# Order of the first layer norm's statistics and of the graph convolution's evacuations in a four-stage graph network kernel

## What is computed

```
L0  h = x @ fc^T + b;  8 Euler steps  h += dt*(alph*0.5*(adj@h - h) + h@w_eff - h + x)
L1  h = relu(adj @ (x @ Wg0 + bg0)); h = relu(adj @ (h @ Wg1 + bg1))
    for p in 1..4: an LSTM over windows of p nodes overwrites every p-th node of h
L2  A_hat = normalised adj; batchnorm(relu(batchnorm((A_hat @ x) @ W1^T + b1)) @ W2^T + b2)
L3  edge attention with 4 heads over 256 edges (segment softmax), then @ W_out^T
```

## Time and profile before

| what | value |
|---|---|
| median of 3 runs | 1010.1 us (1010.0 to 1010.34) |
| profiled execution, its own time | 1015.05 us |
| its span, first to last instruction | 1013.0 us |
| mean granted clock of TensorE | 0.969 |
| HBM traffic | 22.83 MB read, 7.87 MB written |

### The profile page before, as it was taken

One profiled execution on the slowest core, in us unless ns is written; L12 is line 12 of the kernel. 1 busy time (PEld: TensorE's weight loads), 2 busy tenths in 40 slices (PEclk: granted clock), 3 DMA queues, 4 the chain that ended last, 5 costly groups with the idle time before them and its releaser, 6 DMA issues. The chain is left out here.

```text
span 1013.0 us, 14415 instructions
## 1 busy us (share of the span) xinstructions
PE 926.2 (91%) x5120; PEld 795.4 (79%) x5120; DVE 671.9 (66%) x1662; ACT 538.4 (53%) x1112; POOL 309.3 (31%) x284
## 2 busy tenths in 40 slices
PE   6999997999998999998999999899999978588984
PEld 4689986899997898997889899787788853365763
DVE  6665435445546657655755675697887876779887
ACT  2043324664645565554565564557567548366644
POOL 3011222332323233232323333314333220155742
PEclk9989999999999999999999999999979998799987
DMA  8030011001010100101010001201100000000014
GB/s 223 1 81 17 7 63 63 1 22 42 1 42 2 42 22 1 42 2 42 1 42 21 29 15 35 89 1 63 42 1 22 2 0 1 0 1 1 0 44 123
DMA packets 33995, 31.62 MB, mean 31 GB/s; under 512 B 8451, under 2 KB 28035, under 8 KB 33925
## 3 DMA queue, kind: packets, MB, share of 16 engines
q1 hardware_dynamic: 32900, 30.64, 9.9%
q10 hardware_dynamic: 960, 0.07, 0.1%
q0 software_dynamic: 64, 0.00, 0.0%
HBM read 22.83 MB, written 7.87 MB: 30 GB/s over the span
## 5 line engine op out<-in xcount | busy, mean ns | idle before, releaser
L1322 ACT ACTIVATE gates<-psum,gbias 128x256 f32<-128x256 f32 (+2 forms) x312 | 158.9, 566 | 68.5 <-PE psum L67 64.5
L65 PE MATMUL psum<-LS,WI 128*128 128x256 f32 (+2 forms) x312 | 105.0, 337 | 8.9 <-ACT gates L1322 5.3
L67 PE MATMUL psum<-LS,WI 128*128 128x256 f32 (+2 forms) x312 | 103.6, 332 | 0.0
L66 PE MATMUL psum<-LS,WI 128*128 128x256 f32 (+2 forms) x312 | 103.6, 332 | 0.0
L72 POOL TENSOR_TENSOR LS<-A,LS 128x512 fp32r<-128x512 f32 (+2 forms) x44 | 49.0, 1114 | 170.7 <-ACT LS L1307 170.6
L72 POOL TENSOR_TENSOR LS<-Hodd,LS 128x512 fp32r<-128x512 f32 (+2 forms) x44 | 48.6, 1103 | 150.4 <-ACT LS L1307 150.4
L72 DVE TENSOR_TENSOR yl<-psum,yh 128x512 fp32r<-128x512 f32 x58 | 39.6, 688 | 65.1 <-ACT yh L1264 44.0
L72 POOL TENSOR_TENSOR XSl<-X,XSh 128x512 fp32r<-128x512 f32 x32 | 42.6, 1334 | 115.9 <-ACT XSh L1259 115.9
L65 PEld LDWEIGHTS psum<-LS,WI 128*128 128x128 f32 x312 | 59.8, 192 | 18.2 <-POOL LS L72 9.9
L1329 ACT ACTIVATE tc<-cell 128x512 f32<-128x512 f32 (+2 forms) x88 | 45.3, 514 | 53.5 <-DVE cell L1617 29.4
L65 PE MATMUL psum<-B2h,LT2h 128*128 128x256 f32 x256 | 72.7, 284 | 1.0 <-DVE X L1435 1.0
(11 more groups left out here) (372 smaller groups left out, 2680.8 us busy)
## 6 DMA issues: line engine op xcount, KB each, us to landing
WI<-lstm_weights SPq DMA_DIRECT2D x14, 512.0 KB, 3.6
WH<-lstm_weights SPq DMA_DIRECT2D x11, 512.0 KB, 4.6
X<-in_x SPq DMA_DIRECT2D x16, 256.0 KB
out<-X SPq DMA_DIRECT2D x16, 256.0 KB, 2.3
lstm_weights<-WI SPq DMA_DIRECT2D x4, 512.0 KB, 2.6
lstm_weights<-WH SPq DMA_DIRECT2D x3, 512.0 KB, 2.7
A<-in_adj SPq DMA_DIRECT2D x4, 256.0 KB, 4.4
z_A<-in_adj SPq DMA_DIRECT2D x1, 1024.0 KB, 5.3
```

Of the source, the lines that this page charges most:

```text
L65: pe.matmul(out, lhs[0], rhs[0], start=start, stop=False)
L66: pe.matmul(out, lhs[0], rhs[1], start=False, stop=False)
L67: return pe.matmul(out, lhs[1], rhs[0], start=False, stop=stop)
L1322: act.activation(gates[:, gate, 0:n], sh.psum[:, gate, 0:n], ACT.Tanh if gate == G else ACT.Sigmoid, bias=gbias[:, p_ - 1, gate:gate + 1]) ...
```

## The change

The statistics of a pair of batches are taken in halves by node chunks: `("st1", q, a, 0)` now covers chunks 0 and 1 of both batches and stands right behind half 0 of "s"; `("st1", q, a, 1)` covers chunks 2 and 3. In each quarter the second half stands between the layer 0 "v" of batch 0 and its relu. "sh1", the apply of batch 2 and its split move ahead of the first layer 1 product; the apply of batch 3 moves behind the second. In quarter 0 the sets 8 and 9 stand behind both layer 0 "v", set 10 behind both layer 1 "v", set 11 behind the layer 0 "v" of batch 3 and set 12 between the layer 1 "v" of batches 2 and 3. At the end of the order, the statistics of batch 3 and "ln2" of quarter 3's second norm move behind L2's product of batch 11.

```diff
         def giant(kind, q, a):
-            return [(kind, q, a, j) for j in (0, 1)] + ([("th", q, a)] if kind == "t" else [])
+            if kind == "t":
+                return [("t", q, a, 0), ("t", q, a, 1), ("th", q, a)]
+            return [("s", q, a, 0), ("st1", q, a, 0), ("s", q, a, 1)]
...
         def first_norm(q, a):
-            return [("st1", q, a, 0), ("st1", q, a, 1), ("ln1", q, a)]
+            return [("st1", q, a, 1), ("ln1", q, a)]
...
-                    applied(q, 1), split(q, 4), back(q, 3), split(q, 5), giant("t", q, 1), mix(q, 0, 0), mix(q, 1, 0),
-                    giant("s", q, 1), weigh(q, 0, 0), first_norm(q, 1), weigh(q, 1, 0), mix(q, 0, 1), applied(q, 2),
-                    applied(q, 3), split(q, 6), mix(q, 1, 1), split(q, 7), weigh(q, 0, 1), weigh(q, 1, 1), mix(q, 2, 0),
-                    split(q + 1, 0) if q < NQ - 1 else [], mix(q, 3, 0), split(q + 1, 1) if q < NQ - 1 else [],
-                    weigh(q, 2, 0), weigh(q, 3, 0), mix(q, 2, 1), mix(q, 3, 1), weigh(q, 2, 1), weigh(q, 3, 1)]
+                     applied(q, 1), split(q, 4), back(q, 3), split(q, 5), giant("t", q, 1), mix(q, 0, 0), mix(q, 1, 0),
+                     giant("s", q, 1), [("v", q, 0, 0), ("st1", q, 1, 1), ("relu", q, 0), ("ln1", q, 1), ("v", q, 1, 0),
+                                        ("relu", q, 1)]]
+            second = [*applied(q, 2), *split(q, 6)]
+            if q == 0:
+                sets = [[("set", n)] for n in range(NSET - SETS_LATE, NSET)]
+                return parts + [sets[0], sets[1], second, mix(q, 0, 1), mix(q, 1, 1), applied(q, 3), split(q, 7),
+                                weigh(q, 0, 1), weigh(q, 1, 1), sets[2], mix(q, 2, 0),
+                                ahead[0], mix(q, 3, 0), ahead[1], weigh(q, 2, 0), weigh(q, 3, 0), sets[3], mix(q, 2, 1),
+                                mix(q, 3, 1), weigh(q, 2, 1), sets[4], weigh(q, 3, 1)]
+            return parts + [second, mix(q, 0, 1), mix(q, 1, 1), applied(q, 3), split(q, 7), weigh(q, 0, 1), weigh(q, 1, 1), mix(q, 2, 0), ahead[0], mix(q, 3, 0), ahead[1],
+                            weigh(q, 2, 0), weigh(q, 3, 0), mix(q, 2, 1), mix(q, 3, 1), weigh(q, 2, 1), weigh(q, 3, 1)]
...
-            for part in rest:
-                parts.append(part)
-                if part and part[0][0] in ("v", "s"):
-                    parts.append([next(late, None)])
-            parts.append(list(late))
+            parts += rest
...
-        order += applied2(q_, 0, 2) + [("xz", z_)] + widened(z_ - 3) + norm2(q_, 2, 4) + aggregated(z_ - 1)
+        order += applied2(q_, 0, 2) + [("xz", z_)] + widened(z_ - 3) + [("st2", q_, 2)] + aggregated(z_ - 1) + [("st2", q_, 3), ("ln2", q_, 2, 4)]
...
-            def first_stats(q, a, b):
-                if b == 0:
-                    dve.wait_ge(S["ring_free"], ring["s", q, a, 1] + 1)
-                ins = norm.take_stats(dve, QB * q + 2 * a + b)
-                if b == 1:
+            def first_stats(q, a, j):
+                dve.wait_ge(S["ring_free"], ring["s", q, a, j] + 1)
+                for b in (0, 1):
+                    for c in range(2 * j, 2 * j + 2):
+                        ins = norm.row_stats(dve, QB * q + 2 * a + b, c)
+                if j == 1:
                     link(ins)
```

More of the change, by code:

```diff
@@ L767, in stages @@
         def stages(q):
-            return [taps(q, 0), split(q, 2), back(q, 0), taps(q, 1), split(q, 3), back(q, 1), giant("t", q, 0),
-                    taps(q, 2), giant("s", q, 0), first_norm(q, 0), back(q, 2), applied(q, 0), taps(q, 3),
-                    applied(q, 1), split(q, 4), back(q, 3), split(q, 5), giant("t", q, 1), mix(q, 0, 0), mix(q, 1, 0),
-                    giant("s", q, 1), weigh(q, 0, 0), first_norm(q, 1), weigh(q, 1, 0), mix(q, 0, 1), applied(q, 2),
-                    applied(q, 3), split(q, 6), mix(q, 1, 1), split(q, 7), weigh(q, 0, 1), weigh(q, 1, 1), mix(q, 2, 0),
-                    split(q + 1, 0) if q < NQ - 1 else [], mix(q, 3, 0), split(q + 1, 1) if q < NQ - 1 else [],
-                    weigh(q, 2, 0), weigh(q, 3, 0), mix(q, 2, 1), mix(q, 3, 1), weigh(q, 2, 1), weigh(q, 3, 1)]
+            ahead = [split(q + 1, j) if q < NQ - 1 else [] for j in (0, 1)]
+            parts = [taps(q, 0), split(q, 2), back(q, 0), taps(q, 1), split(q, 3), back(q, 1), giant("t", q, 0),
+                     taps(q, 2), giant("s", q, 0), first_norm(q, 0), back(q, 2), applied(q, 0), taps(q, 3),
+                     applied(q, 1), split(q, 4), back(q, 3), split(q, 5), giant("t", q, 1), mix(q, 0, 0), mix(q, 1, 0),
[10 more added lines that the diff above has]
+                            weigh(q, 2, 0), weigh(q, 3, 0), mix(q, 2, 1), mix(q, 3, 1), weigh(q, 2, 1), weigh(q, 3, 1)]
         def norm2(q, b0, b1):
@@ L792, in adjacency @@
                     [("xz", 1)]]
+        SETS_LATE = 5
         def with_adjacency(parts):
@@ L824, in prologue @@
             rest = rest[rest.index(giant("t", 0, 1)) + 1:]
-            for part in rest:
-                parts.append(part)
-                if part and part[0][0] in ("v", "s"):
-                    parts.append([next(late, None)])
-            parts.append(list(late))
-            return [item for item in flat(parts) if item is not None] + [("H", 0, 0)]
+            parts += rest
+            assert sum(item[0] == "set" for item in flat(parts)) == NSET
+            return flat(parts) + [("H", 0, 0)]
         WORK = {"xt": 43, "y": 68, "b": 156, "t": 272, "s": 272, "c": 68, "r": 43, "at": 43, "wt": 43, "a": 68, "w": 68}
```

## The result

| | kernel before | changed kernel |
|---|---|---|
| median | 1011.29 us | 1007.59 us |
| shortest to longest, 20 runs each | 1009.88 to 1019.97 | 1001.43 to 1009.75 |
| profiled execution, its own time | 1015.05 | 1006.18 |
| its span, mean granted clock | 1013.0, 0.969 | 1004.2, 0.972 |

The ratio is 0.9954, with 0.9940 to 0.9967 as its 95% interval: faster, by 3.7 us in the medians and 4.7 by the ratio, where 9.0 were forecast. 1007.59 lies outside the range of 997.2 to 1006.2. Yet the profiled execution took nearly the predicted time (span 1004.0, own time 1006.05). Both things need an explanation.

A forecast was written before the change was run, and what follows sets the result against it. PE was taken as the bound, busy 926 of 1013 us, so only its pauses count: 3.5 + 2.3 + 2.3 + 0.1 + 0.8 = 9.0 us off 1010.1 gave 1001.1 us, with an 8-in-10 range of 997.2 to 1006.2.

The forecast's parts named there:

- Quarter 0, 3.5 us: Quarter 0: first layer 0 product of batch 2 starts at 160.0 instead of 163.53, despite a new 1.9 us pause at v0'.
- Quarters 1 and 2, 2.3 us each: Quarters 1 and 2: c1 1.5 us early, X17's pause gone (1.0), less 0.2 for XSl: 2.3 us each.
- X17's pause: Quarter 1: X17's 0.86 us wait goes, one apply instead of two preceding step 16's gates on ACT; worth 1.0 with overlap.
- The subtracted 0.2 us for XSl of batch 3: Quarters 1 and 2: batch 3's apply behind L17 makes XSl ready about when PE wants it; 0.2 us deducted.
- the stretch at 479.1: TensorE at 1.2 instead of 2.4 GHz from 479.1 to 482.5 behind pauses; its going would gain up to 1.7 us more.
- Quarter 3, 0.1 us: Quarter 3: half statistics not hidden, c0 later; c1's 0.45 us pause and v1's wait (worth 0.5) go: sum 0.1 us.
- The end, 0.8 us: Second norm and L2: batch 11's product w starts 1.75 us early, batch 10's statistics limit the gain to 0.8 us.
- That rival, priced at 1006.2: Clock falls again or longer at v0's new pause or a shifted one: 9.0 - 5.1 = 3.9 us gained, 1006.2; chance 0.10.
- The base: Whole kernel: profiled execution 4.95 us above the median of runs shown; same difference taken off, giving 1010.1 us as start.
- C17's delay: Quarters 1 and 2: batch 3's apply delays C17 by 1.6 us, gain becomes later waits; only 4.4 us, 1005.7; chance 0.12.
- The port: Quarters 1 and 2: relu1's low part beside POOL's split, sharing DVE's second read interface; 0 or 0.5 us each, taken as nothing.

The follow-up runs named there:

- the statistics whole: Changed kernel with all eight statistics again between v0 and its relu, everything else as changed: 1010.3 us, ratio 0.9982 to the kernel before.
- quarter 0 as before: Changed kernel with quarter 0's sets, statistics and applies in the order of the kernel before, the rest as changed: 1008.1 us, ratio 0.9972 to the kernel before.

## Why the prediction was wrong

The waits that the prediction worked out moved as it said; its price for the clock was wrong. By its own steps:

- **Quarter 0, 3.5 us.** The pauses fell as worked out (0.41, 2.13 and 2.01 us became 0.19 and 1.81), and the sets are hidden behind sums and relus where it was said. At full clock the stretch would give 3.5; it gave 2.0 in the profile, because the clock fell behind v0'.
- **Quarters 1 and 2, 2.3 us each.** X17's pause is gone and 0.20 us are left of c1's, a little better than forecast. The subtracted 0.2 us for XSl of batch 3 is the mis-sized term: it costs 0.55 us plus the usual 0.16, so 0.7, and each quarter is worth 1.8. The prediction priced the stretch at 479.1 at up to 1.7 us; its going gave 0.5.
- **Quarter 3, 0.1 us.** 0.4 without the stretch. A longer first pause and no second one, as forecast, and again the fall of the clock behind it (1.6 us) was not.
- **The end, 0.8 us.** 0.8 measured.
- **The clock: here the prediction failed.** It put further falls at nothing in the sum and gave them a chance of 0.10, because the pauses of 2.0 and 2.1 us at that place had brought none in its one profile. With like clocks the parts come to 3.5 + 1.8 + 1.8 + 0.4 + 0.8 = 8.3 us, and the many executions agree (6 to 9). But both profiled executions of the changed kernel have a fall behind v0' and one behind c0 of quarter 3, 1.5 and 1.6 us, and the mean clocks suggest the same for most others. Filling these two pauses gave 3.9 us with no wait shorter. Changing the order so that one of them goes or shrinks gave 4.5 and 2.4, of which some 2 each lie at the place itself. That rival, priced at 1006.2, should have been the likeliest, with some 3 us for two falls instead of 5.1 for one long one. Of the 5.3 us by which the gain fell short (9.0 forecast, 3.7 measured), 0.7 are the parts, 3.1 the two falls, and 1.5 were not located.
- **The base.** 1010.1 was the median of three runs that agreed to 0.34 us. Twenty runs gave 1011.29 and reach to 1020: the three lay in the lowest group. I took the profiled execution's 4.95 us over them as a constant and subtracted it from the changed kernel as well. But that execution had a mean clock of 0.969, where those near 1010 us have 0.976, and the changed kernel's profiled execution lies 1.4 us under its median. The base accounts for 1.2 us of the missed time.
- **The other rivals.** C17's delay didn't turn the gain into later waits, though in the run that moved XSl's split the chain did take back about half of what was moved. The port wasn't put to the test, and that is luck: relu1's low part starts at 303.48 in quarter 1, 0.2 us behind the end of POOL's split. It took 0.68 to 0.69 us everywhere, but in neither kernel did it ever run beside such a split, so the prediction's reason for taking nothing, that it ran 0.68 us in every quarter shown, said little.

The Trainium skill (TensorE: Matmul & The Clock Gate, section "What's actually happening") says that a gate sets the clock by how busy TensorE has been, and that its window runs freely and doesn't restart with the kernel. The executions fit this: one and the same kernel spans 999.4 to 1007.6 us, with granted clocks of 0.977 to 0.969, and the same pauses brought a fall in one profile and none in another. The Trainium skill (TensorE: Matmul & The Clock Gate, section "HAM oscillation — how this bites in real kernels") tells of matmul loops that wait for a DMA, and advises an order of the loop that keeps the clock up. Here DVE and ACT ended the pauses, and both the fillings and the changed orders kept the clock at 1.00 in the windows shown.

What stays open: what decides whether a pause brings a fall. 1.8 us at v0' brought one in four profiles and none in a fifth (the statistics whole), 3.15 us in quarter 3 brought one in four and none in a fifth (quarter 0 as before), and 2.1 and 2.0 us in quarter 0 of the kernel before brought none. Which execution fell where is seen for the profiled ones only; of the others only the mean clock is known. Where the typical executions with quarter 0 as before lose their time wasn't located, nor the 1.5 us above. The stretch near 725 to 735 us was not removed in any run, as the filling began behind the pause.

## What to carry to other kernels

A pause of the engine that bounds the kernel costs its idle time and, as two places here show, can cost a stretch at half clock behind it: price a change that makes or lengthens a pause with both, as a chance, since the same pause doesn't bring it in every execution. A stretch costs half its length only where PE has no later pause that takes it up: the one at 479.1 cost 0.5 of 1.7 us. Before you read a few per cent from two traces, compare their granted clocks and stages, and take a baseline from many executions. Idle matmuls are a cheap test, and a cheap remedy, if they begin inside the pause: look up which wait ends it, put them ahead of that wait, and make sure that PE is there early enough to run them.

## What the runs showed that I had not expected

- Fourteen idle matmuls ahead of one product, in a pause that stays 5 us long, shorten a stage to 33.2 us, from 34.8 to 35.9 in three profiles without them, and the whole kernel's median by 4 us (1002.05 to 997.93, six runs each, in two chip jobs, so the size is loose).
- The spread between executions of one program on one core goes mostly with the clock: about 1 us for each 0.001 of the mean, though at one mean clock (0.970) the changed kernel still spans 1004.6 to 1007.6. It is 8 us from the shortest to the longest of the changed kernel, 10.6 for the kernel before (1009.49 to 1020.08 in one job).
- DVE's statistics overlap a little: four instructions took 0.86 us, although one is recorded with 278 ns on average, and eight took 1.62.
